# Seven of 196 groups of source rows gathered by matrix products on TensorE, the others by GpSimd, in a two-layer graph network

## The reference

```python
msgs = z[edge_dst] @ Wd + z[edge_src] @ Ws + edge_weight[:, None] * ww[None, :] + bm
agg = jax.ops.segment_max(msgs, edge_dst, num_segments=n)
agg = jnp.where(deg[:, None] > 0, agg, 0)
hidden = jax.nn.relu(z @ W1a + agg @ W1b + b1)
x1 = layernorm(z + hidden @ W2 + b2)
# second layer, with mean = segment_sum(h[src], dst) / max(deg, 1)
h = relu(mean(x1) @ W1l.T + b1l + x1 @ W1r.T)
out = layernorm(x1 + mean(h) @ W2l.T + b2l + h @ W2r.T)
```

## Time and profile before

| | |
|---|---|
| median of 3 runs | 1157.37 us (1156.93 to 1158.87) |
| the profiled execution: span | 1155.3 us; 2.1 us below the median of the runs, about what lies around the first and last instruction |
| busy | TensorE 962.4, VectorE 841.5, GpSimd 773.5, ScalarE 402.1 us |
| granted TensorE clock, mean | 0.920 |

### The profile page before, as it was taken

One profiled execution on the slowest core, in us unless ns is written; L12 is line 12 of the kernel. 1 busy time (PEld: TensorE's weight loads), 2 busy tenths in 40 slices (PEclk: granted clock), 3 DMA queues, 4 the chain that ended last, 5 costly groups with the idle time before them and its releaser, 6 DMA issues.

```text
span 1155.3 us, 22138 instructions
## 1 busy us (share of the span) xinstructions
PE 962.4 (83%) x6127; PEld 714.5 (62%) x6127; DVE 841.5 (73%) x2938; ACT 402.1 (35%) x1248; POOL 773.5 (67%) x829
## 2 busy tenths in 40 slices
PE   5787787777887887887887969887889899899997
PEld 4465566566665665655666656666556577566776
DVE  6597677767777867776877777777688878846455
ACT  3343333333332423332332323333323233302664
POOL 6677777777777777777777777777777777200332
PEclk9898878888898989798997989998999999999999
DMA  8533333434333443334443334433344354355321
GB/s 209 147 91 85 96 86 87 99 93 102 88 95 94 102 102 89 93 83 116 101 109 85 92 95 124 112 85 96 91 112 125 98 139 110 89 162 165 89 61 42
DMA packets 122171, 119.47 MB, mean 103 GB/s; under 512 B 24626, under 2 KB 106658, under 8 KB 122039
## 3 DMA queue, kind: packets, MB, share of 16 engines
q1 hardware_dynamic: 94074, 65.78, 21.6%
q0 software_dynamic: 24864, 50.97, 18.4%
q10 hardware_dynamic: 3101, 1.21, 0.4%
HBM read 104.00 MB, written 13.88 MB: 102 GB/s over the span
## 4 chain that ended last, share of the span: by engine, by line
POOL 47%; PE 24%; issue 17%; DVE 6%; DMA 4%; SPq 2%; ACTq 0%; ACT 0%; DVEq 0%
POOL area L953 47%; PE bank L1771 6%; PE bank L1633 5%; PE bank L1571 2%; PE bank L1736 2%; PE bank L1512 2%; PE bank L1561 1%; DMA area<-parts_d 1%; PE bank L1551 1%; PE bank L1722 1%; PE bank L1591 1%; PE bank L1500 1%; DVE area L1122 1%; DVE area L1138 1%; DMA adj_w<-in_dst_dram 1%
## 5 line engine op out<-in xcount | busy, mean ns | idle before, releaser
L953 POOL DMA_INDIRECT area<-zs_d,area x757 | 721.8, 953 | 236.6 <-issue 231.6
L1138 DVE TENSOR_TENSOR_SCAN area<-area,bank 128x512 f32<-128x512 bf16 x196 | 250.0, 1276 | 222.1 <-PE bank L1512 211.0
L808 ACT CAST adj_w<-bank 128x325 f32 x391 | 176.0, 450 | 634.7 <-PE bank L1571 593.2
L1122 DVE TENSOR_SCALAR area<-area 128x325 bf16<-128x325 f16 x782 | 248.6, 318 | 0.0
L1571 PE MATMUL bank<-area 128*128 128x104 f32 x1564 | 248.0, 306 | 0.2 <-ACT area L814 0.2
L1512 PE MATMUL bank<-ident,area 128*128 128x128 f32 x762 | 137.7, 308 | 116.5 <-DMA area<-zs_d,area 116.5
L1571 PEld LDWEIGHTS bank<-area 128*128 128x128 f32 x1564 | 218.7, 216 | 11.6 <-ACT area L814 0.7
L1121 DVE TENSOR_SCALAR area<-area 128x128 bf16<-128x128 f16 x782 | 212.6, 272 | 0.0
L1512 PEld LDWEIGHTS bank<-ident,area 128*128 128x128 f32 x762 | 87.7, 151 | 168.0 <-DMA area<-zs_d,area 141.2
L1561 PE MATMUL bank<-area 128*128 128x325 bf16 x782 | 166.3, 331 | 11.7 <-DVE area L1123 11.6
L1633 PE MATMUL bank<-adj_w,area 128*128 128x512 bf16 (+4 forms) x525 | 114.1, 358 | 19.8 <-DMA area<-parts_d 7.9
(11 more groups left out here) (160 smaller groups left out, 860.8 us busy)
## 6 DMA issues: line engine op xcount, KB each, us to landing
area<-mask_d SPq DMA_DIRECT2D x195, 128.0 KB
area<-zs_d,area POOLq DMA_INDIRECT x757
area<-zs_d SPq DMA_DIRECT2D x640, 0.5 KB
area<-parts_d SPq DMA_DIRECT2D x20, 384.0 KB, 7.5
area<-wp_d SPq DMA_DIRECT2D x195, 9.0 KB
zr_d<-area SPq DMA_DIRECT2D x24, 128.0 KB
area<-zr_d SPq DMA_DIRECT2D x6, 512.0 KB, 4.8
area<-scale_d SPq DMA_DIRECT2D x11, 256.0 KB, 4.2
```

Source lines behind the costliest of these rows:

```text
L808: nc.scalar.copy(adj[:, :, bass.ds(at, W)], A_BANK[s % 2][:, 0:COLS].rearrange("p (h w) -> p h w", w=W))
L953: pool.indirect_dma_start(gring[:, g % GR * 4 + s % 2 * 2 + u, :], None, x if g < RAW else zs_d[0:N, :], bass.IndirectOffsetOnAxis(ap=firs ...
L1122: nc.vector.tensor_scalar(hot_d[:, r, u, :], i_key[:, 0:COLS], key_n[:, u, s:s + 1], None, ALU.is_equal)
L1138: nc.vector.tensor_tensor_scan(S[:, g % 2, 0:n], mask[:, g % MR, 0:n], T_BANK[g % 2][:, 0:n], S[:, (g + 1) % 2, 511:512] if g else 0.0, AL ...
```

## The change

Seven groups, those in `PICKED` (17, 28, 37, 48, 60, 80, 93), are not gathered by GpSimd. `load_sources` brings the whole table `zs_d` into the still unused late columns of `adj_w`. ScalarE and VectorE split each value into a high part in the four-byte format `float32r` and the remainder in the same format (`high_part`, `low_part`, in slots 3 to 5). For a picked group, the 512 source numbers are broadcast to all partitions (`load_key`), turned to floats by ScalarE (`key_to_float`) and to 2-byte floats by VectorE (`key_of`). Then, for each of the 25 rows of 128 nodes, VectorE compares them with the node numbers (`make_hot`, 512 columns, written as `float32r`, a ring of `HOTS` = 4) and TensorE adds two products, table part times one-hot, in `L_BANK` (`pick_rows`). The 25 steps are spread over the slots ahead of the group: each pair (g, a) in `PICKS` says that group g's steps lie in slots a to g - 1. In slot g the weight's share is added in the same bank, and the scan reads that bank. Some semaphores are shared to make room, and a check that such an input fits the scheme is added to the head of the program.

```diff
+PICKS = ((17, 7), (28, 17), (37, 28), (48, 37), (60, 50), (80, 71), (93, 85))
+SPLITS = ((3, 0, 8), (4, 8, 16), (5, 16, 24), (5, 24, NT))
+HOTS = 4
+def hots(k):
+    return [(i, h) for i, (g, a) in enumerate(PICKS) if a <= k < g
+            for h in range(NT * (k - a) // (g - a), NT * (k - a + 1) // (g - a))]
...
+                def load_sources():
+                    sp.wait_ge(nat_sb, 7)
+                    sp.wait_ge(wc_sb, 1)
+                    sp.dma_start(zs_raw[:, 0:NT - 1, :], tiled(zs_d, 0, NT - 1)).then_inc(l_zs, 16)
+                    sp.dma_start(zs_raw[0:LASTN, NT - 1, :], zs_d[(NT - 1) * P:N, :]).then_inc(l_zs, 16)
...
                 for k in range(NG + 5):
                     if 2 <= k < NG:
                         load_edges(k)
+                    if k == 2:
+                        load_sources()
+                    for i, (g, a) in enumerate(PICKS):
+                        if k == a - 4:
+                            load_key(i)
...
+                def high_part(n, h0, h1):
+                    act.wait_ge(l_zs, 32)
+                    k = size(h0)
+                    nc.scalar.copy(zs_high[n][0:k], zs_raw[0:k, h0:h1, :]).then_inc(zs_high_sb, 1)
...
             def gathers(g):
+                if g in PICKED:
+                    return
...
+                def low_part(n, h0, h1):
+                    dve.wait_ge(zs_high_sb, n + 1)
+                    k = size(h0)
+                    nc.vector.tensor_tensor(zs_low[n][0:k], zs_raw[0:k, h0:h1, :], zs_high[n][0:k].bitcast(f32), ALU.subtract).then_inc(zs_low_sb, 1)
+                def key_of(i):
+                    dve.wait_ge(key_float, i + 1)
+                    nc.vector.tensor_scalar(keys[i % 2], key_w, float(CENTER), None, ALU.subtract).then_inc(keyed, 1)
+                def make_hot(i, h):
+                    u = NT * i + h
+                    dve.wait_ge(keyed, i + 1)
+                    if u >= HOTS:
+                        dve.wait_ge(hot_used, u - HOTS + 1)
+                    nc.vector.tensor_scalar(hot_r[u % HOTS], keys[i % 2], node_c[:, h:h + 1], None, ALU.is_equal).then_inc(hot_made, 1)
...
+                    for i, h in hots(k + 1):
+                        make_hot(i, h)
...
+                if g in PICKED:
+                    nc.tensor.matmul(L_BANK[:, :], ww9[0:9, :], wp9[:, g % WR, 0:n], start=False, stop=True).then_inc(t_ps, 1)
+                    return
...
+                def pick_rows(i, h):
+                    u, n = NT * i + h, size(h)
...
+                    pe.wait_ge(hot_made, u + 1)
+                    at = [b for b, (_, h0, h1) in enumerate(SPLITS) if h0 <= h < h1][0]
+                    for part_of in (zs_high[at], zs_low[at]):
+                        last = nc.tensor.matmul(L_BANK[:, :], part_of[0:n, h - SPLITS[at][1], :], hot_r[u % HOTS][0:n, :],
+                                                start=h == 0 and part_of is zs_high[at], stop=False)
+                    last.then_inc(hot_used, 1)
...
+                    for i, h in hots(k):
+                        pick_rows(i, h)
```

More of the change, by code:

```diff
@@ L49 @@
 WIDE = 8
+PICKS = ((17, 7), (28, 17), (37, 28), (48, 37), (60, 50), (80, 71), (93, 85))
+PICKED = tuple(g for g, _ in PICKS)
+CENTER = 1562
+SPLITS = ((3, 0, 8), (4, 8, 16), (5, 16, 24), (5, 24, NT))
+HOTS = 4
+ROW = AW // 2
+SPARE = 801
 NODES = "a source node, which is below N"
@@ L113, in landings, with picked_before @@
 def landings(g):
-    return sum(4 - (i in OWN) for i in range(g % GR, g + 1, GR))
+    return sum(0 if i in PICKED else 4 - (i in OWN) for i in range(g % GR, g + 1, GR))
+def hots(k):
+    return [(i, h) for i, (g, a) in enumerate(PICKS) if a <= k < g
+            for h in range(NT * (k - a) // (g - a), NT * (k - a + 1) // (g - a))]
+def picked_before(k):
+    return max([g for g in PICKED if g < k], default=-1)
 def supers(g):
@@ L191, in gnn_kernel @@
         bm_c, b1_c, c0_c, b1l_c = cols[:, 0:1], cols[:, 1:2], cols[:, 2:3], cols[:, 3:5]
+        node_c = sb("node_c", [P, NT])
+        adj_at = -(-nc.sbuf_base // 32) * 32
         adj_w = sb("adj_w", [P, AWORDS])
@@ L202, in gnn_kernel, with spare @@
             (bf16, 3, BB, SB), (bf16, BB, SB),
-            (i32, 512), (i32, BB), (f32, BB), (i32, BB), (f32, BB), (f32, 5, BB), (f32, 5), (f32, F), (f32, F),
-            (f32, F), (f32, F), (bf16, 3, F), (bf16, 2), (f32, BB))
+            (i32, 512), (i32, BB), (f32, BB), (i32, BB), (f32, BB), (f32, 6, BB), (f32, 5), (f32, F), (f32, F),
+            (f32, F), (f32, F), (bf16, 3, F), (bf16, 2), (f32, BB), (i32, NT))
+        high_at, low_at = ROW - 2 * F, ROW - F
+        zs_raw = adj_w.rearrange("p (h n) -> p h n", n=ROW)[:, :, low_at:ROW]
+        zs_r = [nc.alloc_sbuf_tensor_at(f"zs_r{n}", [P, (h1 - h0) * ROW], f32r, offset=adj_at + 4 * h0 * ROW)[:, :]
+                .rearrange("p (h n) -> p h n", n=ROW) for n, (_, h0, h1) in enumerate(SPLITS)]
+        zs_high = [z[:, :, high_at:low_at] for z in zs_r]
+        zs_low = [z[:, :, low_at:ROW] for z in zs_r]
+        def spare(row, n, lead=0):
+            return slice(row * ROW + SPARE + lead, row * ROW + SPARE + lead + n)
+        key_i = adj_w[:, spare(0, 512)].bitcast(i32)
+        key_w = adj_w[:, spare(1, 512)]
+        keys = [adj_w[:, spare(2, 256, 256 * i)].bitcast(f16) for i in range(2)]
+        hot_r = [nc.alloc_sbuf_tensor_at(f"hot_r{i}", [P, 512], f32r, offset=adj_at + 32 * ((ROW * (5 + i) + SPARE) // 8))[:, :]
+                 for i in range(HOTS)]
         AREA = 15776
@@ L1650, in half_piece @@
                         last.then_inc(piece_ps, 1)
+                def pick_rows(i, h):
+                    u, n = NT * i + h, size(h)
+                    if h == 0:
+                        g, a = PICKS[i]
+                        pe.wait_ge(zs_low_sb, len(SPLITS))
+                        pe.wait_ge(raw_sb, RAW)
+                        if i:
+                            pe.wait_ge(scanned, PICKED[i - 1] + 1)
+                        before = len([p for p in PIECES if p[0] < a])
+                        if before:
+                            pe.wait_ge(acc_sb, before)
+                        rows = len([d for d in DEGREE_SLOTS if d < a])
+                        if rows:
+                            pe.wait_ge(deg_sb, rows)
+                    pe.wait_ge(hot_made, u + 1)
[4 more added lines that the diff above has]
+                    last.then_inc(hot_used, 1)
                 def drain_piece(h0, h1):
```

41 lines of the change are left out of this document (36 added, 5 removed).

## The result

The changed kernel takes 1146.9 us (median, 1145.45 to 1148.36), the kernel before 1157.2 in the same comparison: a ratio of 0.9908, 95% interval 0.9892 to 0.9924. That is a gain of about 10 us, where 20 were forecast. The profiled execution has a span of 1143.6 us, against 1155.3 of before: 11.7 us less, of which 10.3 lie before the last gather's end.

The account below looks back on a forecast made before the run. GpSimd's indirect gathers were taken as the bound, 5.03 us a group. Of 35 us spared, gains of 6 + 15 - 1 = 20 us were to remain: span 1135.3, median 1137 us, range 1124 to 1161 us.

Parts of the forecast that it names:

- The 35 us that the removal is worth: On GpSimd, 7 groups of 4 gathers removed, 28 x 1.258 = 35.2 us; nothing can bring more.
- The comparison's price: On VectorE, each of 175 comparisons lasts 0.48 us and takes 0.40 us of the queue, 0.44 with collisions.
- Rival 2: VectorE's comparison runs at about one column a nanosecond, 0.70 us with collisions: 1171 us, slower; chance 0.11.
- TensorE's products hide: Products at 0.217 us each, 76 us in all, 1.1 us a slot; 4.4 us a slot stays below VectorE's need.
- rival 3: TensorE becomes the bound: at 1.2 GHz a slot with steps takes 7.3 us, eight such take the gain away; chance 0.03.
- The start: Table load of 1.57 MB delays ScalarE, and with it TensorE and VectorE, by 7 us (4 to 14).
- VectorE's slots and the ring: VectorE needs 3.70 us a slot plus 0.44 a comparison; of 20 us spared by four groups, 14 go into ring waits.
- A count: Sign in the changed profile: gathers 729 in place of 757, said to include those of x.
- Half as much again of comparisons adds 2 us at most: Against rival 4: gathers beside 2.1 us of comparisons a slot lose 0.05 us a slot, so new ones add little.
- Rival 4: VectorE's comparisons hold up GpSimd's gathers, 0.27 us each, 47 us against 35.2 spared: 1169 us; chance 0.03.
- a mean gather above 1 us: Sign in the changed profile, on GpSimd, that the forecast would be wrong.
- Rivals 1 and 5: 1: whole 35 us arrive (0.10); 5: start far above 14 us or steps and scans lock, 1150 to 1160 us (0.07).

Follow-up runs that it names:

- e1_both: Changed kernel with GpSimd gathering all 196 groups again, table load, comparisons and products kept but unused: 1180.3 us, ratio 1.019 to the kernel before.
- e2_no_compare: Changed kernel without the comparisons after the first four, products run on old one-hots, wrong rows: 1129.4 us, ratio 0.9767 to the kernel before.
- e3_psum_compare: Changed kernel with comparisons after the first four reading 256 columns from PSUM, not 512 from SBUF, wrong rows: 1133.5 us, ratio 0.9799 to the kernel before.

## Why the prediction was right in sign and half off in size

**The 35 us that the removal is worth** held: 33 us between e1_both and the changed kernel.

**The comparison's price** held: it lasts 0.496 us (0.48 forecast), and a pair takes 0.87 and three 1.26 us, so the next follows 0.39 us later (0.40 forecast). Rival 2, one column a nanosecond, is out.

**TensorE's products hide**: held. The clock went from 0.86 to 0.97 while the waits for gathers shrank, and rival 3 is out. Line 1775 is busy 94.1 us for 326 in the stretch, 0.29 us each and more than the 0.217 taken from the last stage. That figure was read too low: the row of line 1771 mixes three widths, and its 512-column form alone is busy 43.5 us for 180, 0.242 each. e2_no_compare shows that the products hide all the same.

**The start** held in size: 7 us forecast; GpSimd has 6.5 us of extra idle in the changed kernel and 4.2 without comparisons. The way differs in part. ScalarE was to wait 1 to 11 us for the table, and didn't: its first split at 60.22 follows its last copy. TensorE waited 1.87 us for weights that stand behind the table, VectorE 1.71 us for ScalarE's split, and TensorE's clock was 0.88 in place of 0.97. How the 7 us divide among these wasn't measured.

**VectorE's slots and the ring** were mis-sized. Forecast was 4.8 us a slot in slots 7 to 47 and 14 us of waiting up to slot 60; measured are scans 4.60 us apart from slot 10 to 47, and next to no waiting after slot 9. That VectorE would be full there held (167.3 us busy of the 170 from scan 10 to scan 47). Two things were off. The base of 3.70 us a slot was too high; the 3.56 of the earlier trace rows was the better one, and 3.56 + 2.5 x 0.42 = 4.61, with 0.42 for one of a row of three. And GpSimd, slowed itself, never ran far enough ahead to be stopped. Where it isn't slowed, in e3_psum_compare with VectorE just as full, the waits are only 3.4 us in the long stretch. So beyond the start this term was 3.4 us at most. Group 48's scan came 2.3 us later than before (264.67 against 262.37), not 5 to 10.

**A count** in the prediction was misread: the 757 and 729 gathers are those from `zs_d` alone, and the 20 of x come on top. The sum doesn't use it.

**The step that failed** is "Half as much again of comparisons adds 2 us at most". It measured 18.5 us. The reasoning was that the comparisons of before, 2.1 us of each slot, cost a gather 0.013 us over its 0.940 or so, and that the new ones would do the same in proportion. But the comparisons of before are short (0.25 to 0.30 us mostly) and have 25 to 325 two-byte columns; the new ones have 512 columns, last 0.48 us and stand in rows of two or three. The damage isn't proportional to length: a gather that meets one at the wrong moment waits for its end, and more of a long one is left to wait for. Rival 4 named the mechanism with a price of 0.27 us a comparison and a chance of 0.03. The price was 18.5 / 175 = 0.106 us. The prediction's own sign of it came true: a mean gather above 1 us (1.002 in 100 to 500 us).

The two errors cancel in part. The forecast had 15 us lost of the 35.2, all as GpSimd's waits for the ring (14, the start's 7 among them, and 1); measured are 6.5 us of waits, all at the start, and 18.5 us of longer gathers, 25 in all. So the time lies inside the range by another term than the one forecast, and that is luck. Rivals 1 and 5 are out as well: the 35 us did not arrive, and nothing locks.

The Trainium skill (SBUF — State Buffer, Who interferes with whom) says that a tensor_scalar in a two-port mode and GpSimd exclude each other for the whole instruction, and that GpSimd is then kept from writing its descriptors. The direction agrees with the runs: at the same place a gather takes 1.14 us beside two comparisons of SBUF and 0.95 beside two that read PSUM. The size does not follow from the rule alone: a whole comparison of 0.48 us for each of 175 would be 84 us, and 18.5 were lost. The ends found above, 0.82 and 0.12 us after a comparison's, suggest more: a gather of 0.94 us can be held at two points of its course, with 0.82 and with 0.12 us of it left, by a comparison that began before it came there, and it goes on when that one ends. One that ends earlier or begins later costs it nothing. This is inferred from the times of starts and ends, and leaves the 20 other long gathers open.

## What to carry to other kernels

When work is moved off the engine that sets the pace, price what the new work does to that same engine through what they share, and not only whether its own engine has room. A rate of collisions read from short instructions doesn't scale to long ones or to rows of them; look at single instructions of the engine that sets the pace, and at what ends just before they do. And where such work must be there, keep it from standing in rows (4 us here by the medians), make it narrow in bytes (11 us), or let it read from PSUM (13 us, in a kernel that didn't give the right rows).

## What the runs showed that was not expected

An indirect gather of 0.940 us can have a whole SBUF-to-SBUF comparison of 0.48 us beside it and keep its time (0.95 in the mean of 28), and takes 1.13 us in the mean if 0.2 to 0.4 us of one are still to run when it starts, 1.9 at most beside rows of them. A comparison of 512 columns from two to two bytes lasts 0.357 us and two of them 0.60, from two to four bytes 0.486 to 0.496 and 0.87; one that reads 256 four-byte columns from PSUM lasts 0.471 us and leaves the gathers alone.

On two chips there was a time in which the kernel before took 1393 us in place of 1157, with a granted clock of 0.84 in place of 0.91. The traces of the changed versions from that time have gathers of 963 to 994 ns, no longer than at the usual pace, but waits of up to 10 us that no record explains. What set it apart stays open.
